# Second mixture of experts: tiles turned four at a time, outputs in pairs, scores applied before the scatter

## The reference

```
logits = x @ w_router.T                       # x: normalised rows, 4096 x 128
_, top_idx = top_k(logits, 1)
scores = sigmoid(logits) * one_hot(top_idx)
masked_inputs = scores.T[:, :, None] * x      # scaled by the score before the expert
gate, up = split(masked_inputs @ gate_up_proj, 2)      # per expert, 128 -> 2 * 256
expert_out = (up * silu(gate)) @ down_proj             # 256 -> 128
shared = silu(x @ w_gate.T) * (x @ w_up.T) @ w_down.T
out = x_before_the_norm + shared + expert_out
```

## Time and profile before

| what | us |
|---|---|
| timed runs, median of 3 | 844.25 |
| timed runs, lowest and highest | 844.01, 845.23 |
| profiled execution, first to last instruction (span) | 913.6 |
| TensorE busy in the profiled execution | 839.1 |
| loop over tiles in it, first gate/up product to last down product, about | 88 |

### The profile page before, as it was taken

One profiled execution on the slowest core, in us unless ns is written; L12 is line 12 of the kernel. 1 busy time (PEld: TensorE's weight loads), 2 busy tenths in 40 slices (PEclk: granted clock), 3 DMA queues, 4 the chain that ended last, 5 costly groups with the idle time before them and its releaser, 6 DMA issues.

```text
span 913.6 us, 31471 instructions
## 1 busy us (share of the span) xinstructions
PE 839.1 (92%) x11905; PEld 715.4 (78%) x11905; DVE 600.8 (66%) x1729; ACT 553.3 (61%) x1221; POOL 474.1 (52%) x575
## 2 busy tenths in 40 slices
PE   8998888878899998999999999999999998888786
PEld 3666555546589987998998998998999998867686
DVE  8886677734565647887777777677777676424343
ACT  4886676535387775776665666666666652225463
POOL 6333323463614436786656656655654444544455
PEclk9998999978799998999999999999999999999999
DMA  5455553513534432333553001001000002343330
GB/s 155 137 160 155 157 158 120 154 39 137 195 100 131 129 99 88 107 116 79 175 200 141 24 24 31 24 26 31 23 25 20 12 2 65 115 154 96 92 104 25
DMA packets 84148, 87.37 MB, mean 96 GB/s; under 512 B 15057, under 2 KB 70552, under 8 KB 83234
## 3 DMA queue, kind: packets, MB, share of 16 engines
q1 hardware_dynamic: 74946, 68.11, 24.7%
q0 software_dynamic: 8256, 17.01, 6.0%
q10 hardware_dynamic: 800, 0.24, 0.1%
HBM read 43.13 MB, written 40.44 MB: 91 GB/s over the span
## 4 chain that ended last, share of the span: by engine, by line
PE 81%; DVE 9%; issue 4%; ACT 2%; another core or an unknown queue 1%; DMA 1%; POOL 1%; SPq 0%; ACTq 0%; DVEq 0%; POOLq 0%
PE of L1367 8%; PE sf L1321 7%; PE jf L1242 6%; PE sf L1630 5%; PE sf L1283 4%; PE sf L1559 4%; PE mf L1269 4%; DVE cmx L2004 4%; PE jf L1251 3%; PE sf L1547 3%; PE sf L1458 3%; PE sf L1251 3%; PE of L1080 3%; PE sf L1033 2%; PE mf L1348 2%
## 5 line engine op out<-in xcount | busy, mean ns | idle before, releaser
L882 POOL TENSOR_TENSOR pl<-pT,ph 128x512 bf16<-128x512 f32 x128 | 146.1, 1165 | 105.1 <-DVE ph L2272 101.2
L806 POOL DMA_INDIRECT buf<-gu,slots x64 | 63.8, 996 | 88.9 <-PE of L1169 38.4
L2278 DVE TENSOR_REDUCE cmxb<-mf 128x8 bf16<-128x1024 f32 x64 | 78.2, 1222 | 43.6 <-PE mf L1348 39.2
L1700 ACT ACTIVATE pTf<-sf 128x1024 f32<-128x1024 f32 x64 | 62.6, 1022 | 36.6 <-PE sf L1040 18.0
L2004 DVE TENSOR_REDUCE cmx<-mf 128x8 bf16<-128x1024 f32 x64 | 78.1, 1220 | 10.0 <-PE mf L1061 6.8
L1818 ACT ACTIVATE pT<-sf 128x1024 f32<-128x1024 f32 x64 | 66.6, 1041 | 25.1 <-PE sf L1331 25.1
L1321 PE MATMUL sf<-qTs,kTs 64*128 64x128 f32 x1024 | 75.0, 286 | 1.6 <-ACT pT L1818 1.6
L871 POOL DMA_INDIRECT gb<-eo,slots x64 | 64.9, 1014 | 19.0 <-issue 18.9
L971 POOL DMA_INDIRECT out<-rows x47 | 46.3, 984 | 50.7 <-DVE rows L2677 39.7
L1321 PEld LDWEIGHTS sf<-qTs,kTs 64*128 64x128 f32 x1024 | 62.6, 188 | 7.1 <-issue 2.1
L1242 PE MATMUL jf<-wo,oT 128*128 128x128 f32 x496 | 62.9, 280 | 0.0
(11 more groups left out here) (353 smaller groups left out, 2725.4 us busy)
## 6 DMA issues: line engine op xcount, KB each, us to landing
buf<-zero SPq DMA_DIRECT2D x12, 516.0 KB, 7.1
rows<-buf SPq DMA_DIRECT2D x47, 129.0 KB
buf<-zero SPq DMA_DIRECT2D x22, 256.0 KB, 3.8
eo<-zero SPq DMA_DIRECT2D x22, 256.0 KB
ctxT<-in_ctxP SPq DMA_DIRECT2D x24, 192.0 KB, 2.4
rows<-buf SPq DMA_DIRECT2D x71, 64.0 KB
gu<-in_gu SPq DMA_DIRECT2D x4, 1024.0 KB
kept<-kTs SPq DMA_DIRECT2D x6, 512.0 KB
```

What stands on the lines that cost most here:

```text
L882: nc.gpsimd.tensor_tensor(pl[h][:, :, c, :], pT[h][:, :, c, :], ph[h][:, :, c, :], ALU.subtract)\
L2278: nc.vector.reduce_max(cmx1[b % 2][:, :].rearrange("p (r k) -> p r k", r=2)[:, :, 4 * h:4 * h + 4], M1p[:, :, :].rearrange("p r (c k) -> p ...
```

## The change

Four things are changed in the last two stretches.

- The scaling by the score moves from VectorE's loop to ScalarE's `drain`: `scale_rows(b)` after `shared_gate(b + 3)`, before the scatter. The scatter of batch b waits for it as well.
- Tiles are transposed four at a time (a hop), at turn 4g for the group g+1, into one PSUM bank; VectorE copies the bank of 128x512 at once (`take_tiles`) in place of ScalarE's four copies.
- The gate/up products move to turn t and the down products stay at t-4, so the lag between them is four turns in place of two. Weights are copied five tiles ahead into six buffers; the multiplied tiles have eight places. `XRING` grows from 20 to 24.
- Two tiles' down products go to one of three PSUM banks; VectorE adds both residuals in one instruction of 128x256. GpSimd still issues one indirect DMA per tile, but a pair becomes ready together.

```diff
-XRING, YRING, XSEMS = 20, 8, 6
+XRING, YRING, XSEMS = 24, 8, 6
+GROUP, STAGES, YLAG = 4, 6, 4
...
-        g_bank, y_bank = bank[0:4], (of[:, 0:DM], jf[:, 0:DM])
+        g_bank, y_bank = bank[0:4], (pj_bank[1], of[:, :], jf[:, :])
...
                     pool.wait_ge(M1.sy_done, b + 1)
+                    pool.wait_ge(M1.scaled, b + 1)
...
                 for n in range(TILES1):
-                    pool.wait_ge(M1.y_evac, n + 1)
+                    pool.wait_ge(M1.y_evac, n // 2 + 1)
...
+                def tiles_across(g):
+                    need(pe, M1.xt_evac, g)
+                    for t in range(GROUP * g, min(GROUP * g + GROUP, TILES1)):
+                        pe.wait_ge(M1.xs_in[t % XSEMS], 16 * (t // XSEMS + 1))
+                        nc.tensor.transpose(pj_bank[0][:, t % GROUP * P:(t % GROUP + 1) * P], xs1[t % XRING][:, 0:DM],
+                                            ident[:, :]).then_inc(M1.xt_full, 1)
+                tiles_across(0)
+                warm(TILE_WARM, y_bank[0])
+                for t in range(TILES1 + YLAG):
...
+                        pe.wait_ge(M1.staged, t + 1)
+                        pe.wait_ge(M1.xt_evac, t // GROUP + 1)
+                        need(pe, M1.h_done, t - DEEP + 1)
...
+                    if within(t - YLAG, TILES1):
+                        n = t - YLAG
                         e = expert_of(n)
                         pe.wait_ge(M1.h_done, n + 1)
-                        need(pe, M1.y_evac, n - 1)
+                        need(pe, M1.y_evac, n // 2 - 2)
...
+                    if t % GROUP == 0 and t + GROUP < TILES1:
+                        tiles_across(t // GROUP + 1)
...
+                def scale_rows(b):
+                    act.wait_ge(scores_set, 1 if b < NB - QH else 2)
+                    nc.scalar.activation(rows[:, b, 0:DM], rows[:, b, 0:DM], ACT.Copy, scale=rows[:, b, SCORE:SCORE + 1])\
+                        .then_inc(M1.scaled, 1)
...
                     for b in range(3, NB):
                         shared_gate(b)
+                        scale_rows(b - 3)
+                    for b in range(NB - 3, NB):
+                        scale_rows(b)
...
+                for t in range(STAGES - 1):
+                    stage_weights(t)
+                for t in range(TILES1):
+                    if t + STAGES - 1 < TILES1:
+                        stage_weights(t + STAGES - 1)
+                    act.wait_ge(M1.h_full, t + 1)
+                    need(act, M1.h_done, t - DEEP + 1)
+                    nc.scalar.activation(sg1[t % DEEP], g_bank[t % DEEP][:, 0:2 * P].rearrange("p (c n) -> p c n", c=2),
+                                         ACT.Silu).then_inc(M1.h_act, 1)
...
+                def take_tiles(g):
+                    tiles = min(GROUP, TILES1 - GROUP * g)
+                    dve.wait_ge(M1.xt_full, GROUP * g + tiles)
+                    need(dve, M1.h_full, GROUP * (g - 1))
+                    nc.vector.tensor_copy(xsT1[g % 2][:, 0:tiles * P], pj_bank[0][:, 0:tiles * P]).then_inc(M1.xt_evac, 1)
+                take_tiles(0)
+                for t in range(TILES1 + YLAG):
+                    if t < TILES1:
+                        dve.wait_ge(M1.h_act, t + 1)
+                        need(dve, M1.y_full, t - YRING + 1)
...
+                    if t % GROUP == 0 and t + GROUP < TILES1:
+                        take_tiles(t // GROUP + 1)
+                    n = t - YLAG
+                    if within(n, TILES1) and (n % 2 == 1 or n == TILES1 - 1):
+                        first, w = n - n % 2, n % 2 + 1
+                        dve.wait_ge(M1.y_full, n + 1)
+                        for r in range(first, n + 1):
+                            need(dve, M1.y_out[r % YRING], 16 * (r // YRING))
```

More of the change, by code:

```diff
@@ L420, in build @@
         sg1 = [kT[r // 2][:, 2 * (r % 2):2 * (r % 2) + 2, :] for r in range(DEEP)]
-        xsT1 = [xsT[r // 2][:, r % 2, :] for r in range(DEEP)]
+        o1f = o1s[:, :, :].rearrange("p h d -> p (h d)")
+        xsT1 = [o1f[:, g * GROUP * P:(g + 1) * GROUP * P] for g in range(2)]
+        stage1 = stage + [oT[:, 4 * r:4 * r + 4, :].rearrange("p c n -> p (c n)") for r in range(STAGES - DEEP)]
         hT1 = [hT[r // 2][:, :, (r % 2) * P:(r % 2 + 1) * P] for r in range(DEEP)]
+        hT2 = hT1 + [kT[r // 2][:, 4 + 2 * (r % 2):6 + 2 * (r % 2), :] for r in range(DEEP)]
         ysb1 = [rows[:, XRING + r, 0:DM] for r in range(YRING)]
+        xpair, ypair = rows[:, 0:XRING, DM:2 * DM], rows[:, XRING:XRING + YRING, 0:DM]
         W0 = F0 + 2
@@ L478, in build @@
         odds_done = sem("odds_done")
-        sel_ready, rank_ready = sem("sel_ready"), sem("rank_ready")
+        sel_ready, rank_ready, scores_set = sem("sel_ready"), sem("rank_ready"), sem("scores_set")
         slots_ready = sem("slots_ready")
@@ L1614, in _ @@
                 pe.wait_ge(M1.sy_done, NB)
-                for t in range(TILES1 + 4):
+                def tiles_across(g):
[7 more added lines that the diff above has]
+                for t in range(TILES1 + YLAG):
                     if t < TILES1:
@@ L1618, in _ @@
                             pe.load(expert[t // 4 % 3], tei[0:1, t:t + 4])
[L1619 to L1628, removed]
+                        pe.wait_ge(M1.staged, t + 1)
+                        pe.wait_ge(M1.xt_evac, t // GROUP + 1)
+                        need(pe, M1.h_done, t - DEEP + 1)
                         for c in range(4):
-                            last = nc.tensor.matmul(g_bank[n % DEEP][:, c * P:(c + 1) * P], stage[n % DEEP][:, c * P:(c + 1) * P],
-                                                    xsT1[n % DEEP], start=True, stop=True)
+                            last = nc.tensor.matmul(g_bank[t % DEEP][:, c * P:(c + 1) * P], stage1[t % STAGES][:, c * P:(c + 1) * P],
+                                                    xsT1[t // GROUP % 2][:, t % GROUP * P:(t % GROUP + 1) * P],
+                                                    start=True, stop=True)
                         last.then_inc(M1.h_full, 1)
-                    if within(t - 4, TILES1):
-                        n = t - 4
+                    if within(t - YLAG, TILES1):
+                        n = t - YLAG
                         e = expert_of(n)
                         pe.wait_ge(M1.h_done, n + 1)
-                        need(pe, M1.y_evac, n - 1)
+                        need(pe, M1.y_evac, n // 2 - 2)
                         for f in range(2):
-                            last = nc.tensor.matmul(y_bank[n % 2], hT1[n % DEEP][:, f, :],
+                            last = nc.tensor.matmul(y_bank[n // 2 % 3][:, n % 2 * P:(n % 2 + 1) * P], hT2[n % YRING][:, f, :],
                                                     dn[:, bass.ds(e, 1), f, :].squeeze(1),
@@ L1959, in stage_weights @@
                     e = act.snap(expert[t // 4 % 2][t % 4], min_val=0, max_val=E1 - 1)
[L1960 to L1976, removed]
+                    need(act, M1.h_full, t - STAGES + 1)
+                    nc.scalar.copy(stage1[t % STAGES], gu[:, bass.ds(e, 1), :].squeeze(1)).then_inc(M1.staged, 1)
+                for t in range(STAGES - 1):
[7 more added lines that the diff above has]
+                                         ACT.Silu).then_inc(M1.h_act, 1)
             @block.vector
@@ L2483, in scores_of @@
                     link(nc.vector.tensor_scalar(v2[:, c], v2[:, c], 1.0, None, ALU.add))
-                    link(nc.vector.reciprocal(rows[:, c, SCORE], v2[:, c]))
+                    nc.vector.reciprocal(rows[:, c, SCORE], v2[:, c]).then_inc(scores_set, 1)
                 def drain():
@@ L2654, in _ @@
                 drain()
[L2656 to L2670, removed]
-                                                ALU.mult).then_inc(M1.h_done, 1)
-                    if within(t - 4, TILES1):
-                        n = t - 4
-                        dve.wait_ge(M1.y_full, n + 1)
[L2675 to L2678, removed]
@@ new lines, in take_tiles @@
+                def take_tiles(g):
[8 more added lines that the diff above has]
+                        need(dve, M1.y_full, t - YRING + 1)
+                        nc.vector.tensor_tensor(hT2[t % YRING], sg1[t % DEEP],
+                                                g_bank[t % DEEP][:, 2 * P:4 * P].rearrange("p (c n) -> p c n", c=2),
+                                                ALU.mult).then_inc(M1.h_done, 1)
+                    if t % GROUP == 0 and t + GROUP < TILES1:
[3 more added lines that the diff above has]
+                        first, w = n - n % 2, n % 2 + 1
+                        dve.wait_ge(M1.y_full, n + 1)
+                        for r in range(first, n + 1):
+                            need(dve, M1.y_out[r % YRING], 16 * (r // YRING))
+                        nc.vector.tensor_tensor(ypair[:, first % YRING:first % YRING + w, :],
+                                                y_bank[first // 2 % 3][:, 0:w * P].rearrange("p (t d) -> p t d", t=w),
```

(1 more changed line is left out.)

## The result

| | median of the timed runs | ratio to the kernel before, 95% interval |
|---|---|---|
| kernel before, same comparison | 844.13 us (843.41 to 845.23) | 1 |
| kernel after | 848.21 us (847.48 to 850.19) | 1.0053 (1.0038 to 1.0068) |

The change costs 4.1 us, clear of noise. The forecast was 847.9 us, slower with a chance of 0.49.

What follows compares the result with a forecast made beforehand. TensorE was taken to bound the loop at 1.45 us a tile in timed runs. Terms 0.95 + 0.9 - 0.3 - 1.0 + 3.1 = +3.65 us on 844.25 gave 847.9 us; stated range 836 to 851.

Steps and rivals of the forecast that it cites:

- TensorE sets the rhythm: Expert-tile loop: TensorE's 13 records take 1.45 us a tile, other engines less; 47 x 1.45 = 68 us is the floor.
- difference of 69.4 us: Whole kernel: profiled execution 69.4 us longer than a timed run, so nearly all 16 us of loop idle are absent when timed.
- sum of idle time: Whole kernel: TensorE idles 74.5 us in the profile; only 5.1, at most 31 us, can remain in a timed run.
- Scatters, +0.95: Before the loop: GpSimd's scatters wait for the later scaling, so the loads start 0.95 us later, bounds 0 to 1.3.
- Start, +0.9: Start of the loop: the first product waits for four tiles and their bank copy, 0.9 us later, bounds 0.7 to 1.1.
- Tail, +3.1: End of the loop: GpSimd ends 6.85 us behind TensorE's last product instead of 3.75, costing 3.1 us, bounds 2.3 to 3.6.
- Ramp and stalls, -0.3 and -1.0: Loop: tile 4's transpose no longer waits for scaling, -0.3 us; more slack removes stalls left in timed runs, -1.0 us.
- Rival 1: Loop: stalls are real in timed runs and deeper lookahead removes them; 832.9 us, or 841 if half are real; chance 0.28.
- Rival 2: Loop: stalls are real but GpSimd's outputs set the rhythm; -4.3 against +4.65 us gives 844.6, no change; chance 0.14.
- Rival 3: Loop: a hop finds its tiles missing; 0.5 us at each of 11 hops adds 5.5 us, 853 us; chance 0.05.
- rule on grouping: Loop: grouping helps saturated engines; VectorE, busy 38.59 of 88 us, is not, so this grouping is the wrong way round.

Runs made afterwards that it cites:

- early scaling: Kernel after with batch b scaled right behind the SiLU of batch b+1, not b+3: 0.9985; the 844-level profile was of a version with three further edits, 1.0014.
- both undone: Kernel after with down products two turns behind gate/up, not four, and outputs added and released one by one, not in pairs: 1.0030 of the kernel before, in two comparisons.
- single edits: Kernel after with only outputs one by one, or only a lag of two turns: each 1.0026 of the kernel before, in the comparison at 904.7 us.

## Why the prediction was right, step by step

- *TensorE sets the rhythm, and the loop is full in timed runs.* Right for the kernel after at the level of 844: 67.75 us, no idle time, so more slack could give nothing. For the kernel before it is not shown there, as it has no profile at that level. **The reason that I gave was wrong.** I took the difference of 69.4 us between span and median for something that only the profiled execution has. The same kernel ran at 904.7, 917.7 and 904.4 us in timed runs, and a profiled execution of 904.2 us has such stalls. By all that the runs show, the profile had been taken at one level and the timed runs at the other; the sum of idle time could not tell these apart.
- *Scatters, +0.95.* Too small: the scaling took 0.39 us and not 0.3, and the early scaling shows 1.7 us at the level of 844, outside my bounds of 0 to 1.3. At the level of 905 it is 0.5 to 3.0 us, from 1.9 and 2.5 us to 3.0 to 4.9.
- *Start, +0.9.* From first load to first product 4.82 us against 3.62 and 4.07 in the two profiles before: +0.75 to +1.2, but across the levels. Within the level of 905 it is +1.0 to +1.9 (5.07 to 5.55 us), so the term was rather too small.
- *Tail, +3.1.* The size is right: GpSimd ends 7.3 us behind TensorE (6.85 worked out), 3.9 with both undone (3.75), so 3.4 us. In the timed runs the same two edits give 1.9 us, each ratio with some 1.3 us of uncertainty. Tails of the single edits, 5.35 and 5.5 against 5.4 and 5.15, point to a part for lag and pairing each.
- *Ramp and stalls, -0.3 and -1.0.* Not shown. With the terms as the runs show them, and 0.9 kept for the start, 1.7 + 0.9 + 3.4 = 6.0 us stand against 4.1 measured; some 2 us that the kernel before may lose at this level stay open, as it has no profile there. That my sum came right to 0.3 us is partly luck: two terms too small by 0.8 and 0.3 us were made up for by something that no run shows. My lower end of the range also took -2.5 us for the stalls, where the text gives 0 and -16 as bounds.
- *Rival 1* (slack removes the stalls, 833) did not come at either level: 1.0053 and 1.0004. *Rival 2* (stalls real, GpSimd's outputs set the rhythm, no change) describes the level of 905: stalls remain, ratio 1.0004 (0.9975 to 1.0033). *Rival 3* (tiles missing at a hop) did not come: the transposes wait 0.7 us in all, at the first group.
- By the rule on grouping in the Trainium skill, page "Perfetto Trace Analysis", section "Optimizing Scalar/DVE Operations", the smaller pieces may end sooner, and the tails agree (7.8 against 5.35 us with the addition one by one). By the Trainium skill, page "Perfetto Trace Analysis", section "Summary: the profiler window per engine type", TensorE's end in a profile is an estimate, so that a late signal might have been its own unfinished work. Plain outputs at the level of 905 leave no idle time in the loop with the same products (67.74 us), which speaks against that.

## What to carry to other kernels

When the engine that sets the rhythm is full, as TensorE is here in 67.75 of 67.75 us, more slack behind it gives nothing, and deeper lags and pairs are paid at the end, one by one, by the slowest issuer of outputs. Count what is queued behind the last product before grouping anything. Before explaining why a span and a timed median differ, take a second profile of the same kernel together with the time of that very execution: here it showed that span and median were of different levels.

## What the runs showed of the hardware

- The same program runs at 844 us in some comparisons and at 905 to 918 us in others. In the slow ones the profiles show TensorE's consumers waiting while GpSimd issues indirect DMAs back to back: 5.9 to 16.4 us of TensorE idle time in a loop with 47 of them (ten profiles), none with plain DMAs from ScalarE, and 0 to 0.7 us at the level of 844 with the same 0.98 us for each.
- GpSimd starts an indirect DMA 0.77 to 0.82 us after the end of what it waited for (836.88 to 837.68 in the earlier trace rows), and 0.30 us after the one before when both are ready.
- A ScalarE multiplication by a column of scores, 128x128 from SBUF to SBUF, takes 0.39 us, a copy of the same size out of PSUM 0.27 us.
